# Row copies for every second tile, issued on two queues, and a second attention whose end is re-ordered

## What is computed

```python
q = (x @ Wq_pk).reshape(b, n, P, HEADS, DIM_KEY).transpose(2, 0, 1, 3, 4)
sim = jnp.einsum('pbnhd,pkhd->pbnhk', q, pk_keys)
scores, idx = jax.lax.top_k(sim, PK_TOPK)
idx0 = idx[0]
idx1 = idx[1] * NUM_KEYS
index = (idx0[..., :, None] + idx1[..., None, :]).reshape(b, n, HEADS, PK_TOPK * PK_TOPK)
score = (scores[0][..., :, None] + scores[1][..., None, :]).reshape(b, n, HEADS, PK_TOPK * PK_TOPK)
final_scores, pk_idx = jax.lax.top_k(score, FINAL_TOPK)
final_indices = jnp.take_along_axis(index, pk_idx, axis=-1)
final_scores = jax.nn.softmax(final_scores, axis=-1)
...
k = jnp.einsum('bnhk,bnhkd->bnhd', kv_scores, keys_table[ind])
v = jnp.einsum('bnhk,bnhkd->bnhd', kv_scores, values_table[ind])
sim = jnp.einsum('bihd,bjhd->bhij', q, k)
...
attn = jax.nn.softmax(sim, axis=-1)
out = jnp.einsum('bhij,bjhd->bhid', attn, v)
out = out.transpose(0, 2, 1, 3).reshape(b, n, HEADS * DIM)
return out @ Wo
```

## Time and profile before

| | us |
|---|---|
| median of 3 runs | 2843.3 (2838.46 to 2846.46) |
| profiled execution | 2838.24 |
| its span, first to last instruction | 2836.3 |
| mean granted TensorE clock | 0.932 |

### The profile page before, as it was taken

The page is one execution under the profiler, slowest core; times in us unless marked ns, Lnnn a source line. Parts: engine busy times, 40 slices in busy tenths (PEclk is TensorE's granted clock), DMA queues, the critical chain, the costliest instruction groups (busy, mean ns, idle before and its releaser), DMA issues. The chain is left out here.

```text
span 2836.3 us, 47902 instructions
## 1 busy us (share of the span) xinstructions
PE 2195.5 (77%) x11489; PEld 1773.8 (63%) x11489; DVE 1867.1 (66%) x6336; ACT 783.3 (28%) x2063; POOL 1931.2 (68%) x2033
## 2 busy tenths in 40 slices
PE   6948678887788777886878767877788777877777
PEld 6948556766566556665666655665566655665565
DVE  6689777766666666657566665656666666666541
ACT  5746422221122212221222212221223112221222
POOL 0003767777777777777777777777777777777773
PEclk8969889999999899999899899998999989989999
DMA  4301333333333333333333333333333333333332
GB/s 154 108 1 30 91 95 108 111 108 108 107 111 108 109 108 111 107 108 109 107 110 109 109 107 111 109 110 107 108 110 108 109 108 110 108 109 107 107 108 74
DMA packets 116173, 293.47 MB, mean 103 GB/s; under 512 B 37600, under 2 KB 49248, under 8 KB 113792
## 3 DMA queue, kind: packets, MB, share of 16 engines
q0 software_dynamic: 96816, 264.50, 32.6%
q1 hardware_dynamic: 14880, 23.22, 2.5%
q10 hardware_dynamic: 4144, 2.17, 0.3%
HBM read 288.69 MB, written 1.05 MB: 102 GB/s over the span
## 5 line engine op out<-in xcount | busy, mean ns | idle before, releaser
L321 POOL DMA_INDIRECT ring<-table,rows x2017 | 1923.6, 954 | 707.4 <-issue 578.3
L1565 PE MATMUL ps<-ring,staged 128*128 128x256 f32 x4096 | 995.8, 400 | 191.0 <-DMA ring<-table,rows 169.8
L1565 PEld LDWEIGHTS ps<-ring,staged 128*128 128x128 f32 x4096 | 806.0, 200 | 355.4 <-DMA ring<-table,rows 212.1
L807 DVE RECIPROCAL prec<-psum_row 128x1 f32<-128x1 f32 x128 | 21.0, 164 | 502.1 <-DVEq L806 501.8
L1641 PE MATMUL ps<-s2w,work 128*128 128x128 f32 x2176 | 306.2, 288 | 34.6 <-PEq L1639 33.8
L1177 ACT ACTIVATE work<-ps 128x256 f32<-128x256 f32 x128 | 49.0, 383 | 978.6 <-ACTq L1175 978.6
L1641 PEld LDWEIGHTS ps<-s2w,work 128*128 128x128 f32 x2176 | 274.3, 198 | 64.7 <-issue 61.2
L1610 PE MATMUL ps<-work,qT 128*128 128x512 f32 (+3 forms) x576 | 242.8, 552 | 70.4 <-PEq L1602 67.0
L799 DVE TENSOR_REDUCE nmax<-ps 128x1 f32<-128x128 f32 (+7 forms) x127 | 162.7, 1281 | 204.2 <-DVEq L798 203.5
L792 DVE TENSOR_TENSOR staged<-ps,wgt 128x2048 f32<-128x2048 f32 x128 | 292.0, 2281 | 0.2 <-issue 0.2
L1628 PE MATMUL ps<-ident,work 128*128 128x128 f32 x1088 | 189.8, 298 | 41.9 <-PEq L1551 21.7
(11 more groups left out here) (246 smaller groups left out, 2583.3 us busy)
## 6 DMA issues: line engine op xcount, KB each, us to landing
ring<-table SPq DMA_DIRECT2D x3968, 1.0 KB
ring<-table,rows POOLq DMA_INDIRECT x2017, 2.7
staged<-adj_in SPq DMA_DIRECT2D x16, 1024.0 KB, 4.8
xs<-x_in SPq DMA_DIRECT2D x4, 256.0 KB, 6.6
wpkq<-w_pkq ACTq DMA_DIRECT2D x7, 128.0 KB
out<-xs SPq DMA_DIRECT2D x1, 832.0 KB, 4.8
keyd<-pk_keys ACTq DMA_DIRECT2D x14, 32.0 KB
wo<-w_o ACTq DMA_DIRECT2D x7, 64.0 KB, 2.0
```

Source lines behind the costliest of these rows:

```text
L321: nc.gpsimd.indirect_dma_start(ring[:, t % RING, k, :], None, table_d, bass.IndirectOffsetOnAxis(ap=rows[:, t % ROWS, k:k + 1], axis=0),). ...
L1565: ins = m.matmul(to, diag(t)[:, k, :], ring[:, t % RING, k, :], start=(k == 0), stop=(k == TOPK - 1))
```

## The change

1. **Copies for every second tile.** `by_rows` becomes t in (0, 2, ..., 14), except tiles up to 4 in head 0. SyncE issues the copies for partitions 0 to 79 (loads of 32, 32 and 16 numbers), ScalarE those for 80 to 127 in two parts: 24 in step t - 3 and 24 in step t - 2 of tile t; of these 12 behind softmax and ahead of kv_out, and 12 at the end of the step. So ScalarE issues 24 copies in each step. The offsets have three buffers, the copies three semaphores.
2. **exp_best** moves from the start of the next step to the end of the step, ahead of the second 12 copies.
3. **Start.** Head 0's step 0 is written out: spread(1) stands ahead of elu_out(4), weigh(3) ahead of normal(4); on ScalarE exp_best(3) ahead of kv_out(0), project_out(5) and key_out(0) ahead of the last groups; on TensorE project(5), the keys and scores of tile 0 ahead of group(3) and group(4).
4. **End.** VectorE sums tiles 14 and 15 of head 7 itself (`weighted`), block by block, each a product of the rows with a weight plus what is there. Tile 15's attention is taken in two parts: the past (tiles 0 to 14) with its own maximum, softmax and product, while the rows of tile 15 are still coming, and the own block of 128 columns last; two factors join them. Tile 15's sixteenth gather signals a semaphore of its own (last_in). The output leaves in three DMAs.

The diff, cut to its core:

```diff
-LOADED = 32
+LOADS = ((0, 32), (32, 64), (64, 80))
+ACT_FROM = 80
+ACT_LOADED = 24
+BY_ROWS = (0, 2, 4, 6, 8, 10, 12, 14)
 def by_rows(t, first):
-    return t % RING == RING - 1 and not (first and t == RING - 1)
+    return t in BY_ROWS and not (first and t <= AHEAD)
+def buffer_of(t):
+    return BY_ROWS.index(t) % 3
...
-                for c in range(0, P, LOADED):
+                for lo, hi in LOADS:
...
-                        sp.dma_start(ring[c + i:c + i + 1, RING - 1, TOPK - 1, :].bitcast(U8),
+                        sp.dma_start(ring[i:i + 1, t % RING, TOPK - 1, :].bitcast(U8),
...
+            spread(1)
+            elu_out(4)
             weigh(AHEAD - 1)
+            normal(4)
...
+            def weighted(t, q):
+                landed(t, q)
+                for k in range(q * QK, (q + 1) * QK):
+                    w, row = wgt[:, t % 4, k:k + 1], ring[:, t % RING, k, :]
...
+                    if k == 0:
+                        v.tensor_scalar(end_ps, row, w, None, ALU.mult)
+                    elif k < TOPK - 1:
+                        v.scalar_tensor_tensor(end_ps, row, w, end_ps, ALU.mult, ALU.add)
+                    else:
+                        v.scalar_tensor_tensor(kv[:, t, :], row, w, end_ps, ALU.mult, ALU.add).then_inc(kv_full, 1)
+                    v.drain()
...
+            add_out(T - 4)
+            weighted(T - 2, 0)
+            score_max(T - 3)
+            for q in range(1, QUARTERS):
+                weighted(T - 2, q)
+            score_max(T - 2)
+            add_out(T - 3)
+            dve.sem_inc(out_ready, 1)
+            weighted(T - 1, 0)
...
+            v.reduce_max(max_past, ps[:, 4:8, :].rearrange("p b n -> p (b n)")[:, 0:(T - 1) * P], X,
+                         negate=True).then_inc(nmax_full, 1)
+            weighted(T - 1, 1)
+            weighted(T - 1, 2)
+            add_out(T - 2)
+            dve.sem_inc(out_ready, 1)
+            weighted(T - 1, 3)
...
-                if not (last and t >= T - AHEAD + 1):
-                    exp_best((t + AHEAD - 1) % T)
...
                 softmax((t - 1) % T)
+                fetch = fetched(t, first, last)
+                if fetch:
+                    a, lo = fetch
+                    at = row_numbers(a, lo)
+                    fetch_rows(a, lo, at[:ACT_LOADED // 2])
                 if t > 0:
                     kv_out(t)
                 turned_out((t - 1) % T, PARITY[(t - 1) % T])
...
                 key_out(t)
+                if not (last and t >= T - AHEAD):
+                    exp_best((t + AHEAD) % T)
+                if fetch:
+                    fetch_rows(a, lo + ACT_LOADED // 2, at[ACT_LOADED // 2:])
...
+            def last_steps():
+                t = T - 2
+                exponentials()
+                past_scores(t)
+                values(t - 1, PARITY[t - 1], bank1, key=t)
+
+                t = T - 1
+                exponentials()
+                past_scores(t).then_inc(s_full, 1)
+                values(t - 1, PARITY[t - 1], bank1)
+                exponentials()
+                turn_block(t - 1, PARITY[t], 0, t)
+                bank1()
+                for b in range(3):
+                    turn_block(t - 1, PARITY[t], b + 1, t)
+                    sum_block(t - 1, PARITY[t], b)
+                kv_copied()
+                turn_keys(t, ps[:, 0, 2 * P:3 * P])
+                sum_block(t - 1, PARITY[t], 3).then_inc(ot_full, 1)
...
+                own_scores(t)
+                output(t)
+                exponentials()
+                m.transpose(ps[:, 0, 3 * P:4 * P], prob[:, t % 2, t * P:N], ident[:, :]).then_inc(pt_full, 1)
...
+                m.matmul(ps[:, 0, 0:P], kv[:, t, D:2 * D], ptown[:, :], start=True, stop=True).then_inc(ot_full, 1)
...
+                m.matmul(ps[:, 0, P:2 * P], oTown[:, :], wo[:, :], start=True, stop=True).then_inc(proj_full, 1)
```

More of the change, by code:

```diff
@@ L853, in step @@
                     find_second(a)
-                if begun:
-                    score_max((t - 1) % T)
-                if not (last and t == T - 1):
+                score_max((t - 1) % T)
+                if not (last and t == T - 3):
                     spread((t + 1) % T)
@@ L867, in step @@
                     find_all(a, first and t < T - AHEAD)
-                if last and t == T - 1:
-                    v.drain()
-                    dve.sem_inc(out_ready, 1)
             def weigh(t):
@@ new lines, in add_out @@
+            def add_out(t):
+                add_out_1(t)
+                v.drain()
+                add_out_2(t)
+                v.drain()
+            for t in range(T - 2):
+                step(t, False, True)
+            add_out(T - 4)
[7 more added lines that the diff above has]
+            weighted(T - 1, 0)
@@ L1272, in offsets_out, with row_numbers @@
+            def offsets_out(t):
                 act.wait_ge(offs_full, 1)
                 act.sem_inc(offs_full, -1)
-                s.activation(offs[:, :], ps[0:1, 2, 0:P], ACT.Copy, scale=float(ROW_BYTES)).then_inc(offs_sb, 1)
+                s.activation(offs[:, buffer_of(t), :], ps[0:1, 2, 0:P], ACT.Copy, scale=float(ROW_BYTES)).then_inc(offs_sb, 1)
+            table_bytes = table_d.rearrange("r d -> (r d)").bitcast(U8).rearrange("(o n) -> o n", o=1)
+            def row_numbers(t, lo):
+                s.drain()
+                _, at = nc.values_load_multi_w_load_instructions(
+                    offs[0:1, buffer_of(t), lo:lo + ACT_LOADED], engines=(mybir.EngineType.Activation,), min_val=0,
+                    max_val=(HEADS * NKV - 1) * ROW_BYTES,
+                    skip_runtime_bounds_check_because="row numbers are sums of a head's offset and two positions")
+                return at
@@ new lines, in fetch_rows, with fetched @@
+            def fetch_rows(t, lo, at):
+                for i, row in enumerate(at):
+                    act.dma_start(ring[lo + i:lo + i + 1, t % RING, TOPK - 1, :].bitcast(U8),
+                                  table_bytes[:, bass.ds(row, ROW_BYTES)]).then_inc(copied_in[buffer_of(t)], 16)
+            def fetched(t, first, last):
+                for part in range(2):
+                    a = t + AHEAD - 1 - part
+                    if by_rows(a % T, first and a < T) and not (last and a >= T):
+                        return a % T, ACT_FROM + part * ACT_LOADED
+                return None
@@ L1537, in per @@
                 def per(first):
-                    return [16 * (QK - (q == QUARTERS - 1 and by_rows(s, first))) for s in range(t % RING, T, RING)]
+                    return [16 * (QK - (q == QUARTERS - 1 and (s == T - 1 or by_rows(s, first)))) for s in range(t % RING, T, RING)]
                 if first:
@@ L1572, in _ @@
             bank1()
-            sums(0, 0, range(QUARTERS), True)
-            group(3)
-            group(4)
-            pe.wait_ge(bank7_free, 1)
-            pe.sem_inc(bank7_free, -1)
+            sums(0, 0, True)
             def project(t):
@@ L1692, in step @@
                         bank1()
-                    sums(h, t, range(QUARTERS), first)
+                    sums(h, t, first)
                     exponentials()
@@ L1697, in step @@
                 scores(t)
-            for t in range(T):
+            project(AHEAD + 1)
+            kv_copied()
+            turn_keys(0)
+            scores(0)
+            group(3)
+            group(4)
+            pe.wait_ge(bank7_free, 1)
+            pe.sem_inc(bank7_free, -1)
+            for t in range(1, T):
                 step(0, t, True, False)
```

277 lines of the change are left out of this document (163 added, 114 removed).

## The result

| | before | after |
|---|---|---|
| median (range), us | 2842.1 (2838.5 to 2846.5), 4 runs | 2874.7 (2859.9 to 2880.6), 4 runs |
| profiled execution, us | 2838.24 | 2859.86 |
| its span, us | 2836.3 | 2858.1 |
| mean granted TensorE clock | 0.932 | 0.926 |

The change makes the kernel slower, by a ratio of 1.0106 (95%: 1.0064 to 1.0148), where I had forecast 2811 us, 1.1% faster. The time is above my range too.

What follows compares the result with a forecast made beforehand. Gathers set the pace before; after, TensorE's path (276 + 33.5 = 309.5 us a head, gathers 310) likely sets the end. Head 0 to 656, six heads to 2513, then sums and tail: span 2804, + 1.9 + 5.1 = 2811 us; range 2782 to 2870.

Steps and rivals of the forecast that it cites:

- The start: Head 0's reordered steps: GpSimd's hole of 8.0 us at tile 5 shrinks to about 0.8, 7.2 us for the gathers.
- the path: TensorE, ScalarE and VectorE handing work to each other in order: 309.5 us a head after, against the gathers' 310.
- My sign that would tell it: GpSimd's waits for slot_free: small if the path is just level, tens of us if it is the bound.
- the path without copies: A later head's TensorE path, from head 0's trace: 276 us, plus 0.5 for turning row numbers in every second step.
- package one: ScalarE's load of 24 numbers and 12 copies, behind softmax and ahead of kv_out: 13 us a head exposed.
- package two: ScalarE's 12 copies at the end of a step, ahead of project_out: 20 us a head exposed.
- (b): Rival: ScalarE's copies put TensorE's path over the gathers, gain gone from 0.352 us a copy, 2944 us at 0.40; chance 0.17.
- (a): Rival: a copy costs ScalarE its bare 0.22 us, the gathers stay the bound, 2786.5 us; chance 0.2.
- The 50 ns: The skill's figure for the sequencer's dispatch of a DMA; by it 24 copies take 1.2 us a step, hidden.
- (c): Rival: SyncE falls behind and the last copied rows come late, 2854 us at 0.42 us a copy; chance 0.03.

Runs made afterwards that it cites:

- the rulers: Four variants of the changed kernel, blocks 12 and 13 of every tile not gathered from head 1 on, with none, either or both of ScalarE's packages: 2564.2 to 2874.9 us.
- the filling: Changed kernel with unread products ahead of TensorE's waits for ScalarE in heads 1 to 6: 2824.7 us; also with blocks 12 and 13 not gathered: 2811.5 and 2827.9.
- the ruler: Changed kernel without ScalarE's 48 copies and, from head 1 on, without the gathers of blocks 12 and 13: 2564.2 us, head 279.8 us.
- the seven-tile kernel: Changed kernel with seven tiles of a head by rows, 104 copies on SyncE and 24 on ScalarE ahead of its copy of the sums: 2845.7 us.
- 88 and 40 copies: Changed kernel with 88 copies on SyncE and 40 on ScalarE for each of eight tiles, TensorE's idle moments filled: 2785.2 us, ratio 0.9797 to before.

## Why the prediction was wrong, step by step

Right:
- The gathers (1987 of them, 1.25 us apart), the copy on ScalarE (0.338 for my 0.337) and the load (1.67 for my 1.8).
- The start: tile 5's hole is gone and sums(1) starts at 358.2, 8.6 us ahead of my 366.8. Head 0's path behind it took 289.4 us (358.2 to 647.6) for my 289.2. The start and end together gained 19 us in a kernel of their own, as forecast.
- The shape of the bottleneck: "the path, not the gathers, is likely to set the end". My sign that would tell it, tens of us of GpSimd's waits for slot_free, is there: 46 us, up to 12.3 at a time.
- SyncE's 80 copies are in time; TensorE's list has no wait for them.

Wrong: the size of a head's path, 309.5 us for 319.7 (heads 1 to 6: 647.6 to 2565.7). Six heads of that are 61 us. The rest nearly cancels: head 0 ended 8.4 us early (647.6 for 656), head 7 to sums(13) took 232.0 for my 233.5, and the part from there to the end of the span 60.4 for 57.7. So 61.1 - 8.4 - 1.5 + 2.7 = 54 us, which is 2858.1 for 2804. The median is another 10 us off, since it lies 14.9 above this profiled execution and I had assumed 5.1.

The terms of the path, by the rulers (without the filling):

| term | forecast | measured | of it TensorE idle | of it TensorE busy |
|---|---|---|---|---|
| the path without copies, its offsets in it | 276.5 | 279.8 | 44.9 | 234.9 |
| package one, with its load | 13 | 20.4 | 16.8 | 3.6 |
| package two on top of it | 20 | 18.7 | 14.7 | 4.0 |
| sum | 309.5 | 318.9 | 76.4 | 242.5 |

- **The path without copies.** I took 1.7 us off the way from sums(0) to sums(1) as a wait for rows. It was none: in the ruler, where the rows lie ready, sums(0) takes 8.9 us as before instead of 7.1, at a granted clock of 0.81. In sums(2) of heads 2 to 6 are another 2.1 of this kind (9.2 us, clock 0.77), which head 0, my model for all heads, doesn't have. The 2.5 us that I took off head 0 were right: the ruler's head 0 takes 262.6 us from sums(1) on, and I had 262.2.
- **Package one.** 7.4 us too little. Step 10 gave 5.0 us for my 2.4: the wait is 3.5, slower products are 1.5. From sums(15) to the next sums(0) it gave 9.1 for my 5.6: some 6.7 are idle time (4.7 of it the wait for the first turned block, where I had 4.6), and 2.4 slower products. The other steps gave 6.3 for my 5.0, all of it idle time. (By its own holes my 6.6 for steps 4 to 15 should have been 6.3.) So some 4 us are products at half clock, and 3.5 are waits that I sized too small.
- **Package two** was right as a sum by luck: on top of package one its waits are 14.7 us for my 20, and 4.0 of slower products fill the gap in part. By itself with its load it costs 28.1, 19.2 of it idle time and 8.9 slower products, more than half of it in steps 1 to 6; half clock is 40 us a head against the ruler's 17.

The failed step: I added up waits and took every product at the duration that it had in the trace of before, in head 0, with a granted clock of 0.98. A wait put into TensorE's path lengthens the work behind it too. By the rulers the path is 279.8 + 31.5 of the copies' waits + 7.6 of slower products = 318.9. The waits came out 1.5 us under my 33, as package one's error and package two's cancel; the slower products were not in the sum at all; and the base was 3.3 us short, itself for the sake of such products (3.9 us in steps 0 and 2). That is the 9.4 us of a head.

Head 0 alone would have hidden it. There the copies cost 26.8 us (289.4 against the ruler's 262.6) for my 27, and the granted clock stayed at 0.97. In the heads behind it the products are slow from the start: sums(1) to sums(4) of head 3 take 8.1 to 8.7 us, in head 0 sums(2) to sums(6) 7.1 each.

**My rivals.** (b) had the mechanism and the sign: copies put the path over the gathers. But I tied it to one condition, a copy of 0.352 us or more. The copy was 0.338 and the rival came true all the same, since its margin was a path of 313.7, and 3.3 us of that margin were gone from the start with the short base. A chance of 0.17 was too low for a sum that had no term for the clock and ended 0.5 us under the gathers. (a) is out: the copy doesn't cost its bare 0.22. The 50 ns that I set beside it were the wrong figure to compare: the Trainium skill ("DMA: Bandwidth & Descriptors", section "Anatomy of one DMA — SWDGE (gpsimd) path") gives them for DMAs on GpSimd's path, and these are issued by ScalarE and SyncE. Here the median instruction took 228 ns and one followed the other after 338. (c) didn't happen here, and did where SyncE had 104 or 128 copies for tiles two short steps apart.

## What to carry to other kernels

When two limits of a loop come out within a few per cent of each other, measure each one alone before spending the slack between them: take enough of the one's work away that the other must show itself. Price a wait on TensorE's path as the wait and the slower products behind it, and if it can't be avoided, try to fill it with products that nobody reads. And an engine that only has to issue is not free of timing: copies that fit on average were late where the steps were short.

## What the runs showed of the hardware

- **A load into registers depends on where it starts.** ScalarE's loads: 12 numbers 0.96 us, 20 numbers 1.44, 24 numbers 1.67, 18 from byte 368 1.64, all from starts that are multiples of 16 bytes; 18 from byte 440, the only start that isn't one, 4.08. In one kernel the same count from two starts took 1.64 and 4.08 us, so the start matters; that it is the 16 bytes that decide was not tried. Why 18 numbers from byte 368 take longer than 20 was not looked into.
- **Filling idle TensorE time with unused products made the kernel 50 us faster**, and the path 6.9 us a head shorter, with 130 more instructions in TensorE's count (1339 for 1209).
- **Most kernels that the path or late copies hold scatter more.** The changed kernel's 4 runs span 21 us, the 7 of the filled one 23, the 12 of the seven-tile kernel 26, the 8 of the kernel with both packages and fewer gathers 32. Bound by the gathers, 4 runs without copies on ScalarE span 5 us, 4 with package one 3, 5 with 88 and 40 copies 1.4, and 13 of the kernel before 10. But the rulers with no copies and with package two, bound by the path, have 2 runs each, 6 and 1 us apart. One profiled execution says less about the median of the first kind: here 14.9 us less. Why they scatter was not looked into.
